# A decoder layer with two-of-eight experts on one core: 36 slots of half-row granularity, four of them shared by two experts, in place of 39 slots

## The reference, cut to what matters

```python
xn = rms_norm(x, norm_scale)
scores = jnp.einsum('bsd,ed->bse', xn, w_router)            # 8 experts
_, ids = jax.lax.top_k(scores, 2)
c = jnp.take_along_axis(jax.nn.softmax(scores, axis=-1), ids, axis=-1)
h = jnp.einsum('bsd,ehd->bseh', xn, w_up)                   # h is 2 x 704
val, gate = jnp.split(h, 2, axis=-1)
y = jnp.einsum('bseh,edh->bsed', val * jax.nn.silu(gate), w_down)
out = jnp.sum(jnp.take_along_axis(y, ids[..., None], axis=2) * c[..., None], axis=2)
```

## Time and profile before

| | before |
|---|---|
| median of three runs | 421.85 us (420.56 to 421.88) |
| the profiled execution, its own time | 421.26 us |
| its span | 419.4 us |
| TensorE busy | 375.3 us, 89% of the span, 2491 matmuls |
| VectorE busy | 265.6 us, 63% |
| ScalarE busy | 242.4 us, 58% |
| POOL busy | 180.3 us, 43% |
| TensorE's share of the chain that ended last | 71% |
| ScalarE, VectorE, DMA in that chain | 8%, 8%, 4% |
| granted TensorE clock, mean | 0.971 |
| moved by DMA | 47.57 MB |

### The profile page before, as it was taken

How to read it: one execution, slowest core, us unless ns; L and a number is a source line. 1 busy time by engine, 2 the same in 40 slices (tenths; PEclk the granted TensorE clock), 3 DMA queues, 4 the chain that set the end, 5 groups by cost and what they waited for, 6 DMA issues and landing times.

```text
span 419.4 us, 9669 instructions
## 1 busy us (share of the span) xinstructions
PE 375.3 (89%) x2491; PEld 268.6 (64%) x2492; DVE 265.6 (63%) x672; ACT 242.4 (58%) x451; POOL 180.3 (43%) x184
## 2 busy tenths in 40 slices
PE   5699999999998066999899999999999999999981
PEld 5578888888886042566466666666666666666650
DVE  2799678898886986877766664454445445445440
ACT  3499965877765386778556544545444444454440
POOL 2545545765556002346345444334434434433321
PEclk9899999999999659999999999999999999999998
DMA  7999873452225602143243343334334343333411
GB/s 226 404 423 409 317 242 113 135 167 76 76 83 195 193 1 64 28 65 63 53 76 57 57 77 58 68 65 68 58 63 71 55 74 65 55 72 63 63 16 24
DMA packets 45302, 47.57 MB, mean 113 GB/s; under 512 B 25696, under 2 KB 41056, under 8 KB 44128
## 3 DMA queue, kind: packets, MB, share of 16 engines
q1 hardware_dynamic: 37200, 36.28, 26.8%
q0 software_dynamic: 7536, 10.52, 15.9%
q10 hardware_dynamic: 544, 0.52, 0.4%
HBM read 32.83 MB, written 9.50 MB: 101 GB/s over the span
## 4 chain that ended last, share of the span: by engine, by line
PE 71%; ACT 8%; DVE 8%; issue 5%; DMA 4%; POOL 1%; POOLq 0%; SPq 0%; DVEq 0%; ACTq 0%
PE bank L1339 32%; PE bank L1366 5%; PE bank L1390 5%; PE bank L1391 5%; PE bank L1392 5%; ACT arena L464 3%; PE bank L1200 3%; PE bank L1254 3%; PE bank L1263 2%; ACT arena L479 2%; DMA arena<-in_w 2%; PE bank L1142 1%; PE bank L1151 1%; PE bank L1160 1%; PE bank L1158 1%
## 5 line engine op out<-in xcount | busy, mean ns | idle before, releaser
L1339 PE MATMUL bank<-expert_w,arena 128*128 x702 | 152.0, 362 | 3.9 <-issue 1.1
L772 POOL DMA_INDIRECT out<-arena,add_idx x39 | 67.5, 1732 | 128.1 <-ACT arena L646 128.1
L1339 PEld LDWEIGHTS bank<-expert_w,arena 128*128 128x128 f16 x702 | 66.9, 98 | 65.1 <-issue 12.1
L761 POOL DMA_INDIRECT arena<-xrow_hbm,take_idx x39 | 40.0, 1026 | 42.8 <-DVE add_idx L1055 22.6
L1116 DVE SCALAR_TENSOR_TENSOR arena<-bank,dn_small,arena 128x512 f32<-128x512 f32 x78 | 45.3, 580 | 18.5 <-PE bank L1339 15.9
L1103 DVE COPY arena<-bank 128x1024 f16<-128x1024 f16 x39 | 26.9, 690 | 44.0 <-PE bank L1366 44.0
L668 ACT ACTIVATE arena<-arena 128x512 f16<-128x512 f32 x39 | 24.5, 629 | 51.7 <-DVE arena L1116 51.7
L1390 PE MATMUL bank<-expert_w,arena 128*128 x195 | 53.2, 273 | 1.0 <-DVE arena L1103 0.9
L1391 PE MATMUL bank<-expert_w,arena 128*128 x195 | 53.2, 273 | 0.0
L1392 PE MATMUL bank<-expert_w,arena 128*128 x195 | 53.2, 273 | 0.0
L1122 DVE TENSOR_TENSOR arena<-arena 128x512 f16<-128x512 f32 x39 | 27.0, 693 | 28.4 <-ACT arena L668 28.4
(11 more groups left out here) (191 smaller groups left out, 679.4 us busy)
## 6 DMA issues: line engine op xcount, KB each, us to landing
expert_w<-in_wup SPq DMA_DIRECT2D x8, 1408.0 KB, 18.0
expert_w<-in_wdn SPq DMA_DIRECT2D x8, 640.0 KB, 4.7
rows<-in_x SPq DMA_DIRECT2D x8, 256.0 KB, 7.5
arena<-in_ctxT SPq DMA_DIRECT2D x8, 256.0 KB, 3.2
xrow_hbm<-front SPq DMA_DIRECT2D x8, 256.0 KB, 2.3
out<-rows SPq DMA_DIRECT2D x8, 256.0 KB, 2.7
rows<-in_wup SPq DMA_DIRECT2D x1, 1408.0 KB, 6.0
expert_w<-in_wdn SPq DMA_DIRECT2D x16, 64.0 KB, 4.5
```

The costliest lines, as they stand in the source:

```text
L761: pool.indirect_dma_start(out=xs_row[:, i % 2], out_offset=None, in_=xrow_hbm, in_offset=bass.IndirectOffsetOnAxis(ap=take_idx[:, i:i + 1] ...
L772: pool.indirect_dma_start(out=out, in_=yt[:, i % 2], in_offset=None, out_offset=bass.IndirectOffsetOnAxis(ap=add_idx[:, i:i + 1], axis=0), ...
L1339: last = T.matmul(bank[q][:, 0:n], xsT[:, slot, 2 * a + c], up_w[:, ds(w0 + c * UPC + w * 2 * H + lo, n)], start=m == 0, stop=m == len(pro ...
```

## The change

It replaces the slots, where the weights are kept and where they are split.

1. **Slots.** An expert's pairs are rounded to 64 rows. There are 32 uniform slots of one expert and 4 mixed ones; a mixed slot's rows 0 to 63 and 64 to 127 can be of two experts. In a mixed slot each product is two, one for each half, on 64 columns of the array and 64 partitions of the bank; the second half's weights are first copied by DMA to a place of their own. A mixed slot is added to the output by two indirect DMAs, in which the rows of the other half go to padding rows.
2. **Order.** Experts are ranked by their number of full slots, the largest first. `FIRST_SLOT` is the first slot at which the expert of each rank can begin; TensorE waits on constants there.
3. **Weights.** All raw weights are loaded during stages A and B and only squared there. The first-ranked expert is split between routing and slot 0. Every other expert's weights are loaded again from DRAM, by DMAs that ScalarE issues in given steps, and split in the place of its rank.
4. **Around it.** xn is stored from two buffers instead of one; the norm sums are one product; the probabilities are normalized by POOL; the routing has 12 links more up to the slot column and 11 after the table; all engines' slot programs are written out without a loop.

The diff, cut to its core ("..." marks what is left out):

```diff
+EXP = UPC + DNC
+UNIFORM, MIXED = 2 * NT, NE // 2
+NSLOT = UNIFORM + MIXED
...
+        FIRST_SLOT = [0, 4, 7, 11, 14, 18, 21, 25]
+        UP_STEP = {2: (1, 0), 3: (1, 1), 5: (2, 0), 6: (2, 1), 8: (3, 0), 9: (3, 1), 11: (4, 0), 12: (4, 1),
+                   14: (5, 0), 15: (5, 1), 17: (6, 0), 18: (6, 1), 20: (7, 0), 21: (7, 1)}
+        DN_STEP = {3: (1, 0), 4: (1, 1), 6: (2, 0), 7: (2, 1), 9: (3, 0), 10: (3, 1), 12: (4, 0), 13: (4, 1),
+                   15: (5, 0), 16: (5, 1), 18: (6, 0), 19: (6, 1), 21: (7, 0), 22: (7, 1)}
+        FETCH_UP = {1: 1, 2: 2, 5: 3, 8: 4, 11: 5, 14: 6, 17: 7}
+        FETCH_DN = {2: 1, 3: 2, 6: 3, 9: 4, 12: 5, 15: 6, 18: 7}
+        HALF_STEP, MIX_STEP = 24, 27
...
         @block.scalar
...
+            def fetch_up(k, e):
+                act.wait_ge(s_lo, 4)
+                act.dma_start(expert_w[:, (k + 1) * EXP:(k + 1) * EXP + UPC], wup[ds(e, 1)].squeeze(0)).then_inc(s_fup[k], 16)
+
+            def fetch_down(k, e):
+                act.wait_ge(s_dlo, 2)
+                dst, src, tail = raw_dn(k + 1), wdn[ds(e, 1)].squeeze(0), (NH - 1) * D
+                act.dma_start(dst[:, 0:tail], src[:, 0:tail]).then_inc(s_fdn[k], 16)
+                for lo in (0, HLAST):
+                    act.dma_start(dst[lo:lo + HLAST, tail:DNC], src[0:HLAST, tail:DNC]).then_inc(s_fdn[k], 16)
...
+                if r in UP_STEP:
+                    n, c = UP_STEP[r]
+                    up_high(n, c, ranked(n))
                 if live(r, 1, NSLOT):
...
+                if r in DN_STEP:
+                    n, h = DN_STEP[r]
+                    down_high(n, h, ranked(n))
+                if r in FETCH_UP:
+                    fetch_up(FETCH_UP[r], ranked(FETCH_UP[r]))
+                if r in FETCH_DN:
+                    fetch_down(FETCH_DN[r], ranked(FETCH_DN[r]))
+                if r == HALF_STEP:
+                    act.wait_ge(s_lo, 2 * NE + 2)
+                    act.wait_ge(s_dlo, 2 * NE)
+                    for q in range(2):
+                        copy_half_up(q)
+                        copy_half_down(q)
...
         @block.gpsimd
...
-                if i:
-                    pool.wait_ge(s_add, 16 * i)
-                pool.indirect_dma_start(out=out, in_=yt[:, i % 2], in_offset=None,
-                                        out_offset=bass.IndirectOffsetOnAxis(ap=add_idx[:, i:i + 1], axis=0),
-                                        compute_op=ALU.add).then_inc(s_add, 16)
+                for m in range(1 if i < UNIFORM else 2):
+                    if i == UNIFORM and not m:
+                        pool.wait_ge(s_half, 3)
+                    if i or m:
+                        pool.wait_ge(s_add, added(i) + 16 * m)
+                    rows_of = add_idx[:, i:i + 1] if i < UNIFORM else half_idx[:, m, i - UNIFORM:i - UNIFORM + 1]
+                    pool.indirect_dma_start(out=out, in_=yt[:, i % 2], in_offset=None,
+                                            out_offset=bass.IndirectOffsetOnAxis(ap=rows_of, axis=0),
+                                            compute_op=ALU.add).then_inc(s_add, 16)
...
         @block.vector
...
+                if r - 1 in DN_STEP:
+                    n, h = DN_STEP[r - 1]
+                    down_low(n, h, load_expert(slot_expert, UNIFORM + 2 * MIXED + n))
...
+                    if r in UP_STEP:
+                        n, c = UP_STEP[r]
+                        up_low(n, c, load_expert(slot_expert, UNIFORM + 2 * MIXED + n))
...
         @block.tensor
...
+                    if i < UNIFORM:
+                        last = T.matmul(bank[q][:, 0:n], x, split_w[:, ds(home + (c * UPC + at_w), n)], **flags)
+                    else:
+                        T.matmul(bank[q][0:half, 0:n], x[:, 0:half], split_w[:, ds(home + (c * UPC + at_w), n)], **flags)
+                        last = T.matmul(bank[q][half:P, 0:n], x[:, half:P], half_up[(i - UNIFORM) % 2][c][:, at_w:at_w + n], **flags)
```

743 lines of the change are left out of this document (389 added, 354 removed).

## The result

The changed kernel takes **474.7 us** (median of four runs, 473.5 to 478.1) against 421.2 for the kernel before: 1.128 times, 95% interval 1.122 to 1.135. The forecast was 429, with a range of 411 to 442. The sign was right, the size was not: slower by 53.5 us where 7.5 was forecast.

What follows compares the result with a forecast made beforehand. TensorE was taken as the bound of the expert stage, then waiting for ACT and DVE after the change. Terms -2.7 + 1.7 + 7.6 + 3.7 + 3.7 - 6.5 = +7.5 on 421.3 gave 429 us, range 411 to 442.

Steps and rivals of the forecast that it cites:

- Stages before the routing: Stages A and B: squares, splits and waits removed, less small operations added; -2.7 us, bounds -6 to +0.5.
- Routing: From the first routing link to slot 0: more links, partly offset by fewer elsewhere; +1.7 us, bounds +0.5 to +4.
- Slots 0 to 3: First slots: refetch of expert 1, ScalarE's loads and issues, late down weights; +7.6 us, bounds +3 to +12.
- Slots 3 to 22: Nineteen steps with splits, value loads and DMA issues in line on DVE and ACT; +3.7 us, bounds 116 to 130 total.
- The contention rival: Refetched 14.3 MB slow landings beside gathers, transposes and adds; +11 us, 440 us in all, chance 0.11.
- Slots 22 to 31: Nine steps with step 24's loads and issues on ACT and mixed scales on DVE; +3.7 us, bounds -1 to +7.
- The forecast step of about 9: Step at slots 23 to 24: four value loads and six issues on ACT, 5.0 us, 3.2 past the slack.
- Last four slots: Slot 31 to the end: eight serial adds of 4.0 us set the end; -6.5 us, bounds -8 to +9.
- that rival: Mixed slots: column tiles run one after another, 5.5 us more each; +17 us, 446 us in all, chance 0.12.
- my margin of 1.3 slots: Last four slots: the adds' chain covers mixed products that take up to 1.3 of a uniform slot.
- Faster rival: Work beside the slots is free, value loads and issues overlap activations; -11.8 us, some 411 us, chance 0.27.
- sentence on issues: Slots: DMA issue time is usually small; leaving issues out makes parts 3 to 5 about 6 us cheaper, result 423.

Runs made afterwards that it cites:

- e1: Changed kernel with stage B's eight down loads spread out: two before the stage, one behind each context load from batch 2 on; 468.3 us, ratio 1.110.
- e8: Changed kernel with each rank's expert loaded once per engine (ScalarE, VectorE) and kept, and each set of down weights moved by one DMA; 458.8 us, ratio 1.087.
- e2: Changed kernel with ScalarE copying the router's scores before squaring the down weights in stage B, not after; 468.1 us, ratio 1.113.
- e5: Changed kernel with half copies spread one a step over steps 24 to 29, mixed scales half a slot a step over 24 to 31; 467.2 us, ratio 1.108.
- e7: Changed kernel with the mixed slots at 26, 28, 30 and 32 in the order of work instead of last; 469.1 us, ratio 1.114.
- e3: Changed kernel with the expert of each split and fetch fixed when the program is built, so those value loads go; 458.6 us, ratio 1.090.
- e4: Changed kernel without the 28 refetch DMAs and their 14 value loads on ScalarE; 456.0 us, ratio 1.079.
- e10: Changed kernel with both the ranks' value loads and the refetches left out, splits kept; 443.1 us, ratio 1.052.
- b1: Changed kernel with the edits of e1, e2, e5, e7 and e8 together (copies and scales from step 22), refetches moved within the step; 441.9 us, ratio 1.046.
- b5: b4 with small work on ScalarE and VectorE moved to where each waits anyway, and mixed slots one earlier; 414.2 us, ratio 0.982.
- b4: b1 with deeper buffers, gathers issued ahead of adds, and each expert's refetch in three DMAs in three steps; 428.7 us, ratio 1.011.

## Why the prediction was wrong, step by step

1. **Stages before the routing: -2.7 forecast, +9.0 measured; the step that failed first.** Stage B starts at 48.0 to 50.9 instead of 52.1, so what changed in stage A, which I had priced at 0.3 for the squares, was worth 1 to 4; no run takes it apart. But I counted what left the engines and not what moved on SP's queue: eight down loads, paced before by the steps, now stand ahead of the context of batch 2, and in pieces that slow them (e1, e8). And I put the squares in the splits' place on ScalarE without asking who stands behind them (e2). TensorE, which I took as the bound throughout, stood still 4.9 us, ran its next step at a granted 0.50, and lost 1.2 us in each of four later steps. No bound covered this, because I had bounded operations and not their places.
2. **Routing: +1.7, measured +3.1 to take_idx and 0.7 more to slot 0.** Mis-sized, within its bounds.
3. **Slots 0 to 3: +7.6, measured +7.5.** The chain is the one described: issue at 180.8, landing 6.0 later, the split, 10.24 to slot 1's transposes. That the sums agree to 0.1 is partly luck: with the same code there, e1, e2, e5 and e7 took 27.7 to 31.1, which would be +7.9 to +11.3.
4. **Slots 3 to 22: +3.7, measured +19.2.** The mechanism was right (value loads and issues in line on two sequencers) and the size was off fivefold. I priced the loads by DVE's three-step sum and ScalarE's at 1.1 us beyond its slack. Measured, they cost 14.5 and the refetches 12.0, overlapping by 3.8 (e3, e4, e10). Part of it is arithmetic: by my own 0.5 us for each of four loads, VectorE's three steps add up to 19.2 and not 18.5, which would have made +8. The rest is what the loads and issues hold up: TensorE stands still for 14.0 us more than before, mostly for ScalarE (10.3 us of its waits there, for hs_high and for the copy of hT), where I had counted on slack. Behind two of these waits the clock fell as well, some 3 us that I had not priced. And the refetches delayed gathers and adds: TensorE waits 4.0 us for transposed rows. The contention rival (0.11) was part of the truth beside my own case, where I had made them alternatives. I took the 0.38 DMA share as room, but a share is a mean: in the changed kernel the adds of slots 0 to 22 land after 4.7 us beside a refetch (median of 12) and 3.9 otherwise, a gather after 4.6 at most (7.1 in b1, against 2.8).
5. **Slots 22 to 31: +3.7, measured +14.5.** The forecast step of about 9 took 15.9. Value loads beside the copies' traffic take 0.87 to 0.96 instead of 0.28, so the bundle was 9.8 us ahead of ScalarE's next operation instead of 5.0, and the clock fell again. The mixed scales cost 1.4 in each of four steps, not 0.4: two loads with their register steps and six copies are 2.1 us on VectorE ahead of the silu's product.
6. **Last four slots: -6.5, measured +0.2.** The serial chain of eight adds sets the end, as forecast, at 4.8 a piece instead of 4.0; the copies of the last two mixed slots ran beside the first adds. The one row for an add (3.73) was of a quiet time.
7. **The rivals.** The column tiles overlap; that rival is out. The Trainium skill, "TensorEngine Tiling (Array Packing)", Restrictions, says that column tiling disables fast weight load. By the trace a weight load of 128x64 takes 110 ns against 98 for 128x128, and the pair's 216 ns hides it. The trace agrees as far as this row goes, and it costs nothing here. The drain on a change of mode, which the Trainium skill names under Key Properties of that page, is there in the records: 0.1 us a change, as shown above, far less than my margin of 1.3 slots.
8. **Faster rival (411).** Its own terms give 409.5, not 411. Its condition, value loads that overlap, is not met in the changed kernel. b5 shows that it can be met: moving the small work into the gaps took the ratio from 1.011 to 0.982, and the same 36 slots and refetches took 414, but with a fifth of the rank loads, whole sets, deeper buffers and gathers first.

The Trainium skill's sentence on issues weighed in the prediction ("DMA: Bandwidth & Descriptors", Issuing engines are not separate DMA queues: initiating is usually small relative to the DMA) is true of the durations here (0.36 against 6.0), and misled by what it leaves out: the comparison that counts is with the slack of the operation behind it. Its other half, that DMAs started by different engines run on the same 16 engines and interleave, is what the gathers show: 2.8 us (median) in the kernel before, up to 7.1 in b1 beside ScalarE's fetches.

By size, slots 3 to 22 are the largest miss (15.5 us over the forecast), then the front (11.7), slots 22 to 31 (10.8) and the end (6.7).

What stays open: the burst against the bytes (b4), and why the clock fell behind one wait of 1.6 us and not behind another. In the front and in step 24 the clock and the wait were not tried apart.

## What to carry to other kernels

When work is taken off the bounding engine and given to "idle" ones, list for each new instruction (DMA issues and register loads too) what stands behind it on its queue and who waits for that; then put it right behind the operation after which its engine waits anyway. Such placing, with one load a rank, whole-set DMAs, loads paced behind the context, earlier mixed slots and deeper buffers, made the difference between 13% slower and 1.8% faster here. Issue latency-bound gathers ahead of any instruction that waits for a landing; deeper buffers bought nothing before that. And when a stall of over a microsecond is forecast in a stream of matmuls, give the time at the lower clock behind it a place in the bounds: about 1.6 us in two of the steps here, nothing in a third with the same wait.

## What the runs showed that I had not expected

- A register load from SBUF (TENSOR_LOAD) takes 0.27 to 0.31 us as a rule (medians 0.278 on ScalarE, 0.308 on VectorE) and 0.87 to 0.96 while copies between SBUF regions run (354.9 to 362.5 us of the changed kernel); a DMA issue went from 0.5 to 1.27 once there.
- After 1.61 us of standing still TensorE ran 1.2 us at 1.00, then the granted clock was 0.51 for some 2 to 3 us and back at 1.00 by 297.7; after 1.60 us of standing still, three steps earlier, it stayed at 1.00; after 4.94 us it was 0.50 from 69 to 75.
- In b1 a gather's landing grew from 2.8 us (the median before) to a maximum of 7.1 and an add's from 3.9 to 9.2, beside refetches and at a mean DMA share of about 0.6.
- A change between column tiles and full products costs TensorE 0.1 us, and a pair of column tiles nothing over one full product.
- A stream of 640 and 64 KB loads moved 314 GB/s where 768 KB loads of the same weights moved 416, with the DMA engines full in both.
